# Rows spread by DMA instead of PE, skip term and step size folded into the scores

## Time and profile before

| what | value |
|---|---|
| median of 3 runs | 1815.66 us (1814.56 to 1815.7) |
| profiled execution | 1815.06 us, span 1813.0 us, mean granted PE clock 0.984 |
| PE busy | 1716.9 us, 95% |
| DVE busy | 1071.7 us, 59% |
| POOL busy | 638.6 us, 35% |
| ACT busy | 521.5 us, 29% |
| DMA | 16.90 MB, mean 9 GB/s |

### The profile page before, as it was taken

One profiled execution on the slowest core, in us unless ns is written; L12 is line 12 of the kernel. 1 busy time (PEld: TensorE's weight loads), 2 busy tenths in 40 slices (PEclk: granted clock), 3 DMA queues, 4 the chain that ended last, 5 costly groups with the idle time before them and its releaser, 6 DMA issues.

```text
span 1813.0 us, 27884 instructions
## 1 busy us (share of the span) xinstructions
PE 1716.9 (95%) x9266; PEld 1364.8 (75%) x9266; DVE 1071.7 (59%) x3116; ACT 521.5 (29%) x906; POOL 638.6 (35%) x724
## 2 busy tenths in 40 slices
PE   5589999999999999999999999999999999999997
PEld 3468778787787878778787777878778787777875
DVE  5555656656565665656656565665656656565635
ACT  3342322324132242323324222242323324232120
POOL 4534251423425144251423415143251523425130
PEclk9779999999999999999999999999999999999999
DMA  2300000000000000000000000000000000000000
GB/s 72 103 6 1 7 7 7 7 6 1 6 6 6 6 7 0 7 6 6 7 6 1 6 7 6 6 7 6 1 6 6 7 6 1 6 7 7 1 6 6
DMA packets 22310, 16.90 MB, mean 9 GB/s; under 512 B 1661, under 2 KB 18761, under 8 KB 22217
## 3 DMA queue, kind: packets, MB, share of 16 engines
q1 hardware_dynamic: 22216, 15.99, 2.9%
HBM read 11.80 MB, written 4.19 MB: 9 GB/s over the span
## 4 chain that ended last, share of the span: by engine, by line
PE 65%; issue 19%; POOL 6%; DVE 6%; ACT 2%; DMA 0%; POOLq 0%; DVEq 0%; ACTq 0%; SPq 0%
PE exp_bank L218 14%; PE exp_bank L220 14%; PE exp_bank L219 14%; PE mix_bank L709 3%; PE mix_bank L218 3%; POOL Wt L682 3%; PE mix_bank L219 3%; PE mix_bank L220 3%; PE mix_bank L717 3%; PE mix_bank L733 2%; PE row_bank L894 2%; POOL sp_lo L915 1%; POOL Wt L629 1%; DVE Xd L536 1%; PE mix_bank L672 1%
## 5 line engine op out<-in xcount | busy, mean ns | idle before, releaser
L915 POOL TENSOR_TENSOR sp_lo<-fbuf,sp_hi 128x512 fp32r<-128x512 f32 x192 | 247.5, 1293 | 358.1 <-ACT sp_hi L912 357.8
L218 PE MATMUL exp_bank<-sp_hi,w_hi 128*128 128x512 f32 x768 | 307.0, 400 | 8.2 <-DVE acc L1006 8.2
L218 PE MATMUL exp_bank<-w_hi,sp_hi 128*128 128x512 f32 x768 | 305.2, 397 | 2.0 <-POOL sp_lo L956 2.0
L220 PE MATMUL exp_bank<-sp_hi,w_lo 128*128 128x512 f32 x768 | 304.0, 396 | 0.0
L219 PE MATMUL exp_bank<-sp_lo,w_hi 128*128 128x512 f32 x768 | 303.9, 396 | 0.0
L219 PE MATMUL exp_bank<-w_lo,sp_hi 128*128 128x512 f32 x768 | 300.9, 392 | 0.0
L220 PE MATMUL exp_bank<-w_hi,sp_lo 128*128 128x512 f32 x768 | 300.5, 391 | 0.0
L912 ACT CAST sp_hi<-fbuf 128x512 fp32r<-128x512 f32 x192 | 118.8, 619 | 597.1 <-DVE fbuf L900 589.3
L678 DVE TENSOR_TENSOR_SCAN Wt<-mix_bank,ident 128x512 f32<-128x512 f32 x128 | 156.2, 1220 | 131.1 <-PE mix_bank L672 129.4
L682 POOL TENSOR_TENSOR Wt<-Wt,Gm 128x512 f32<-128x512 f32 x128 | 165.6, 1293 | 155.8 <-DVE Wt L678 155.8
L218 PEld LDWEIGHTS exp_bank<-sp_hi,w_hi 128*128 128x128 f32 x768 | 144.6, 188 | 47.5 <-DVE acc L1006 14.8
(11 more groups left out here) (209 smaller groups left out, 2580.5 us busy)
## 6 DMA issues: line engine op xcount, KB each, us to landing
x_in<-in_x SPq DMA_DIRECT2D x16, 256.0 KB, 2.8
result<-acc SPq DMA_DIRECT2D x16, 256.0 KB, 2.3
fbuf<-in_W1T SPq DMA_DIRECT2D x12, 256.0 KB, 3.8
fbuf<-in_W2T SPq DMA_DIRECT2D x12, 256.0 KB, 2.8
Xd<-in_Wzg SPq DMA_DIRECT2D x1, 512.0 KB, 6.0
Xd<-in_Win SPq DMA_DIRECT2D x1, 324.0 KB, 3.9
wout<-in_Wout SPq DMA_DIRECT2D x1, 256.0 KB
Xd<-in_Wz SPq DMA_DIRECT2D x1, 128.0 KB, 4.4
```

The source lines that it names most:

```text
L218: nc.tensor.matmul(ps, s_hi, m_hi, start=start and j == 0, stop=False)
L220: last = nc.tensor.matmul(ps, s_lo, m_hi, start=False, stop=stop and j == n - 1)
L915: sig("xw_lo", PO.tensor_tensor(sp_lo[:, at, :], wide[e % 2], sp_hi[:, at, :].bitcast(F32), ALU.subtract))
```

## The change

- The router weights, the decay rows and their running products are transposed once by PE, written by DMA to small DRAM tensors (`dw_dram`, `dA_dram`, `cum_dram`) and read back by DMA with every partition getting the same row: `expert_weight`, `seg_row`, `start_row`, on SP's queue, into two buffers each. The products at L672, L690 and L894 are gone, and so are the fp32r splits of the rows.
- The DVE instructions that read a spread row from PSUM now read it from SBUF.
- The step size leaves `Xd` and goes into the scores: ACT makes `Gh` = Gm*delta per head, four instructions of 128x128 (`mix_score_step`); POOL scales `ends` by delta.
- The skip term goes into the scores as well: DVE adds D*identity to `Gh` (`mix_score_skip`); the three products with `wxd` are gone.
- `mix_y` of pair q moves behind the first expert of the next pair, the last one behind all experts; the layer norm of the batch before moves from q = 0 to q = 3.
- b2 is laid out for a single product per batch; its rows are loaded by 48 DMAs in the setup, and the ring of expert weights is refilled from `split_expert_weights`.
- SP gets a nop behind each wait.

```diff
-                    wait(DVE, "a_split", b)
-                    sig("Xd", DVE.tensor_tensor(
-                        Xd[:, c, :].rearrange("p (h n) -> p h n", h=H),
-                        bank_of(f"X{c}")[:, :].rearrange("p (h n) -> p h n", h=H),
-                        delta[:, c, :].unsqueeze(2).to_broadcast([P, H, HD]), ALU.mult))
+                    sig("Xd", DVE.tensor_copy(Xd[:, c, :], bank_of(f"X{c}")[:, :]))
...
         def mix_rates(eng, b):
+                sig("ps_dA", PE.transpose(ps[R1, 0:P], a_rows[:, :, :].rearrange("p h c -> p (h c)"), ident[:, :]))
+                sig("dA", AC.activation(dA_t[R1, :], bank_of("dA")[R1, 0:P], ACT.Exp))
+                sig("ecum", DVE.tensor_tensor_scan(cum_t[R1, :], dA_t[R1, :], upper[R1, P - 1:P].to_broadcast([H * NC, P]),
+                                                   1.0, ALU.mult, ALU.mult))
+            if eng is SP:
+                wait(SP, "dA", b)
+                sig("rates_out", SP.dma_start(dA_dram.rearrange("h (c t) -> (h c) t", t=P)[:, 1:P], dA_t[R1, 1:P]))
+                wait(SP, "ecum", b)
+                sig("rates_out", SP.dma_start(cum_dram.rearrange("h (c t) -> (h c) t", t=P), cum_t[R1, :]))
+                wait(SP, "rates_out", b)
+                seg_row(b, 0)
+                seg_row(b, 1)
+                start_row(b, 0)
+                start_row(b, 1)
+
+        def seg_row(b, h):
+            sig(f"seg_in{h % 2}", SP.dma_start(seg_b[h % 2][:, :], dA_dram[h].partition_broadcast(P)))
+
+        def start_row(b, q):
+            wait(SP, "ps_yq", b if q >= 2 else b.prev(), q - 1 if q >= 2 else None)
+            for j in range(2):
+                sig(f"ctd_in{q % 2}", SP.dma_start(ctd[j * NS:(j + 1) * NS, q % 2, :],
+                                                   cum_dram[2 * q + j, P:T].partition_broadcast(NS)))
...
+        def mix_score_step(eng, b, h):
+            G = Gh[h % 2]
+            if eng is AC:
+                wait(AC, "Gm", b)
+                if h >= 2:
+                    wait(AC, "W", b, h - 1)
+                else:
+                    wait(AC, "W", b.prev())
+                for c in range(NC):
+                    last = AC.activation(G[:, c, :], Gm[:, c, :], ACT.Copy, scale=delta[:, c, h:h + 1])
+                sig("G_dt", last)
+
+        def mix_score_skip(eng, b, h):
+            G = Gh[h % 2]
+            if eng is DVE:
+                wait(DVE, "G_dt", b, h + 1)
+                flat = G[:, :, :].rearrange("p c t -> p (c t)")
+                sig("G_skip", DVE.scalar_tensor_tensor(flat, ident4[:, :], d_b[:, h:h + 1], flat, ALU.mult, ALU.add))
...
         def mix_decay(eng, b, h):
-            if eng is PE:
-                sig("ps_seg", PE.matmul(ps[:, :], sel, rows_d[:, :], start=True, stop=True))
-                sig("scan", DVE.tensor_tensor_scan(W, bank_of(f"seg{h}")[:, :], ident4[:, :], 0.0, ALU.mult, ALU.add))
+                wait(DVE, f"seg_in{h % 2}", b, h // 2 + 1)
+                sig("scan", DVE.tensor_tensor_scan(W, seg_b[h % 2][:, :], ident4[:, :], 0.0, ALU.mult, ALU.add))
+            if eng is SP and h + 2 < H:
+                wait(SP, "scan", b, h + 1)
+                seg_row(b, h + 2)
             if eng is PO:
-                sig("W", PO.tensor_tensor(W, W, Gm[:, :, :].rearrange("p c t -> p (c t)"), ALU.mult))
+                wait(PO, "G_skip", b, h + 1)
+                sig("W", PO.tensor_tensor(W, W, Gh[h % 2][:, :, :].rearrange("p c t -> p (c t)"), ALU.mult))
...
         def mix_from_start(eng, b, q):
-                sig("ctd", DVE.tensor_tensor(ctd[:, q % 2, :], bank_of(f"decb{q}")[:, 0:cols], CT[:, P:T], ALU.mult))
+                wait(DVE, f"ctd_in{q % 2}", b, 2 * (q // 2 + 1))
+                sig("ctd", DVE.tensor_tensor(ctd[:, q % 2, :], ctd[:, q % 2, :], CT[:, P:T], ALU.mult))
...
         def mix_y(eng, b, q):
-                mm3(ps[:, :], [(wxd_hi[:, w], wxd_lo[:, w], xT_hi[:, :], xT_lo[:, :])], stop=False)
...
         def route_rows(eng, b):
+                wait(SP, "dwT", b)
+                sig("dw_out", SP.dma_start(dw_dram.rearrange("e (c t) -> (e c) t", t=P), rows[0:E * NC, :]))
+                wait(SP, "dw_out", b)
+                expert_weight(b, 0)
+                expert_weight(b, 1)
...
         def expert_row(eng, b, e):
-                sig("ps_row", PE.matmul(rb[:, :], sel, rows_s[:, :], start=True, stop=True))
-                sig("xw", DVE.tensor_tensor(wide[e % 2], rb[:, :], x1T, ALU.mult))
+                sig("xw", DVE.tensor_tensor(wide[e % 2], row_b[e % 2][:, :], x1T, ALU.mult))
+            if eng is SP and e + 2 < E:
+                wait(SP, "xw", b, e + 1)
+                expert_weight(b, e + 2)
...
         def body(eng, b, front_next, norm_before=True):
             for q in range(NQ):
+                mix_from_start(eng, b, q)
+                experts(eng, p, [e], ahead)
+                mix_score_skip(eng, b, 2 * q + 1)
+                mix_decay(eng, b, 2 * q + 1)
+                if q < NQ - 1:
+                    mix_score_step(eng, b, 2 * q + 2)
+                if q > 0:
+                    mix_y(eng, b, q - 1)
+                experts(eng, p, [e + 1], ahead)
+                if q == NQ - 1 and norm_before:
+                    expert_norm(eng, p.prev())
                 e += 2
                 if q < NQ - 1:
+                    mix_score_skip(eng, b, 2 * q + 2)
                     mix_decay(eng, b, 2 * q + 2)
+                    mix_score_step(eng, b, 2 * q + 3)
-                mix_y(eng, b, q)
             experts(eng, p, range(e, E), ahead)
+            mix_y(eng, b, NQ - 1)
...
         def setup(eng):
+                for e in range(E):
+                    at = B2ROW + e * NC
+                    for c in range(NC):
+                        SP.dma_start(b2_sb[at + c:at + c + 1, c, :], b2[e:e + 1, :]).then_inc(sems["small"], 16)
+                SP.wait_ge(sems["pad"], 6)
+                SP.dma_start(dA_dram.rearrange("h (c t) -> (h c) t", t=P), cum_t[0:H * NC, :]).then_inc(sems["zero"], 16)
...
         def router_product(eng):
+            if eng in (SP, DVE):
+                eng.wait_ge(sems["zero"], 16)
+            if eng is PE:
+                PE.wait_ge(sems["small"], 16 * (5 + E * NC))
```

More of the change, by code:

```diff
@@ L30 @@
 NR = 3
-B2ROW = 32
-DTROW = 64
-LOROW = 32
+WCOLS = 32
+B2ROW = E * NC
 LN_EPS = 1e-5
@@ L115, in layer_program @@
         Gm = sb("Gm", [P, NC, P])
+        Gh = [sb(f"Gh{n}", [P, NC, P]) for n in range(2)]
         Wt = sb("Wt", [P, 2, 2 * T])
@@ L119, in layer_program @@
         ctd = sb("ctd", [P, 2, T - P])
-        rates = ctd[:, :, :].rearrange("p a b -> p (a b)")[:, 0:T]
+        dA_t, cum_t = sb("dA_t", [P, P]), sb("cum_t", [P, P])
+        seg_b = [sb(f"seg_b{n}", [P, T]) for n in range(2)]
         zg = sb("zg", [P, NQ, T])
         dt_s = sb("dt_s", [P, 6, NC * H])
-        delta, a = sb("delta", [P, NC, H]), sb("a", [P, NC, H])
+        delta, a_rows = sb("delta", [P, NC, H]), sb("a_rows", [P, H, NC])
+        a = a_rows[:, :, :].rearrange("p h c -> p c h")
         a_hi, a_lo = sb("a_hi", [P, NC, H], F32R), sb("a_lo", [P, NC, H], F32R)
@@ L178, in layer_program @@
         product("stored", 1, 16)
+        product("dw_out", 1, 16)
+        product("rates_out", 2, 16)
+        for n in range(2):
+            product(f"row_in{n}", E // 2, 16)
+            product(f"seg_in{n}", H // 2, 16)
+            product(f"ctd_in{n}", NQ, 16)
         sems = {n: ctx.enter_context(nc.semaphore("set_" + n)) for n in
                 ("mix_w", "win", "wbdt", "small", "decay_par", "ring0", "ring1", "ring2", "ring3",
-                 "w_hi", "w_lo0", "w_lo1", "masks", "cast", "chain", "chain_d", "alog", "ps_r", "router", "pad")}
+                 "w_hi", "w_lo0", "w_lo1", "masks", "cast", "chain", "alog", "ps_r", "router", "pad", "zero")}
         waited = {}
@@ L566, in mix_rates @@
                 ps = mix_bank(b, "dA")
-                for c in range(NC):
-                    last = PE.matmul(ps[RATES, tok(c)], a[:, c, :], ident[:, :], start=True, stop=True)
-                sig("ps_dA", last)
+                sig("ps_dA", PE.transpose(ps[R1, 0:P], a_rows[:, :, :].rearrange("p h c -> p (h c)"), ident[:, :]))
             if eng is AC:
                 wait(AC, "ps_dA", b)
-                wait(AC, "cum_lo", b.prev())
-                wait(AC, "ps_yq", b.prev())
-                sig("dA", AC.activation(rates[RATES, :], bank_of("dA")[RATES, :], ACT.Exp))
@@ L960, in expert_b2 @@
             if eng is PE:
-                wait(PE, "xw", b)
-                for c in range(NC):
-                    last = PE.matmul(rb[:, tok(c)], rows[:, tok(c)], b2_sb[:, :], start=True, stop=True)
-                sig("ps_b2", last)
+                wait(PE, "dwT", b)
+                sig("ps_b2", PE.matmul(rb[:, :], rows[:, :], b2_sb[:, :, :].rearrange("p c d -> p (c d)"), start=True, stop=True))
             if eng is DVE:
```

216 lines of the change are left out of this document (75 added, 141 removed).

## The result

| | before | after |
|---|---|---|
| median, us | 1815.68 (1814.56 to 1816.82, 4 runs) | 1832.86 (1830.59 to 1834.58, 4 runs) |
| ratio, 95% interval | | 1.0094 [1.0076, 1.0111] |
| span of the profiled execution, us | 1813.0 | 1831.4 |

Slower, inside the range; the forecast moved the time by 8 us, the chip by 17. Most of what was forecast of the head pairs came true. The slowdown itself came from a place where I had written "as late as now", and not from the terms that made the forecast slower.

What follows compares the result with a forecast made beforehand. PE bounds the kernel before; after the change the SBUF port shared by DVE and POOL takes PE's saving back. 1813.0 + 15 x 0.0 + 12 - 2.6 = 1822.4 us span, median 1824, range 1680 to 1860.

Steps and rivals of the forecast that it cites:

- The port: Head pairs: DVE instructions with two SBUF inputs and POOL's exclude each other, so a pair needs 9.2 us; chance 0.57.
- The skip addition's holding of 0.54: Head pairs: each skip addition on DVE keeps POOL off for 0.54 us, taken from the nearest row; 1.07 at the scan's rate.
- PE's saving: Per body: removed row and skip products and shorter ones save PE 9.0 us; a pair would need 7.5 us of PE.
- the rival that PE stays the bound: Head pairs: scans and skips don't hold the port, -7.5 to -10 us per body, 1690 us; chance 0.17.
- DVE restarts as late as now: Start of a pass: DVE was assumed to begin as late as in the kernel before, no change.
- The sum of the body: One pass: -0.8 us, against eight handovers at 0.1 us of semaphore each, gives 0.0; bounds -10 and +4.
- Expert 2 at 664.0, 2.0 us earlier: First stretch of a body: the rates' transposition, 3 row products and the earlier row bring expert 2 about 2.0 us forward.
- Batch 0, +12: Batch 0: b2's loads delay the router's product by 5 to 12 us, four pairs add 4; bounds +3 to +22.
- The last mixture, -2.6: End of the kernel: the last mixture loses 11 row products, -2.6 us.
- The late row: Router row by DMA arrives late, `xw` 0 holds up PE's first expert: +1.5 us a pass, 1847 us; chance 0.17.
- The clock: Head pairs: PE less busy, its granted clock falls to 0.77, +60 us, 1885 us; chance 0.09.
- The signs: Right: slower scans, `xw`, POOL products, PE busy about 85%, period 107; wrong: period below 102, router's product before 33 us.

Runs made afterwards that it cites:

- e6: The changed kernel, with ACT copying the identity once a pass into the router's PSUM bank, where scans and skip additions read it; 1732.55 us, ratio 0.9548.
- e5: The changed kernel with one more small DVE copy in the setup and nothing else; 1815.11 us, ratio 1.0008.
- e2: The changed kernel with two rotating PSUM banks instead of three, the third holding the identity for scans and skip additions; 1813.93 us, ratio 0.9998.
- e3: The changed kernel with two rotating PSUM banks instead of three and the identity still in SBUF; 1903.01 us, ratio 1.0483.
- e4: The kernel before with step size and skip term folded into the scores and outputs one expert later, rows still with PE and PSUM; 1785.81 us, ratio 0.9842.
- e7: The kernel before with one more small DVE copy in the setup; 1813.9 us, ratio 1.0003.
- e1: The changed kernel with expert 2's row sent after the loop's restart instead of just before it; 1830.06 us, ratio 1.0087.
- e9: The changed kernel with four small DVE copies added in the setup; 1816.84 us, ratio 1.0004.

## Why the prediction was right in its course and short in size

- *The port, right.* A pair was priced at 9.2 us and, with handovers, a pass at no change; measured are 9.48 a pair and 47.49 us from expert 2 to the last output, where the hand schedule had 711.3 - 664.0 = 47.3. e6 against e5, and e2 against e3, show the mechanism by taking it away. The skip addition's holding of 0.54, the nearest row's, was good enough: 0.74 us alone.
- *PE's saving, right.* e4 returns the skip products at 0.23 each; e6, freed of the port, has passes of 102.7 us, 5.6 below before, where the rival that PE stays the bound had 7.5 to 10 less. The difference lies in the waits that e6 still has: without PE's waits a pass takes 97.2 us there and 105.7 in before, 8.5 less, where 9.0 were forecast.
- *The step that failed: "DVE restarts as late as now".* In its place the restart took 4.25 us instead of 3.20. It cost 1.0 us in E to T of each of the 12 passes behind a jump back, 4.5 us for the clock in three of them, and 2.1 more at the entry to the loop. e5 prices it: 1832.86 - 1815.11 = 18 us. With it undone, 13 passes last 1.3 us less than before, 0.1 a pass, against the 0.0 of the forecast.
- *The sum of the body, right by luck.* By its own terms it was -0.9 (711.3 against 712.2) - 0.3 + 0.8 for handovers = -0.4 a body, or -6 us in all; I had added -0.9 and -0.3 up to -0.8. Expert 2 then came 0.7 later and B to E 0.4 longer than forecast, which made up for it. (In the last line, too, 1824.5 and 0.6 make 1825 and not 1824.)
- *Expert 2 at 664.0, 2.0 us earlier: too much.* Counted from the transposition it came 1.3 earlier (10.22 us against 11.51), as T to S shows too (-1.25). What kept the other 0.7 I did not isolate.
- *Batch 0, +12: too much; measured +5.5.* Two errors of opposite sign. The loads of b2 were priced by the rows of other loads, at 0.43 to 0.60; they took 0.30, and the router's product came 3.7 us earlier instead of 5 to 12 later. The four pairs cost more: from the router's product to the first E 92.8 us instead of 83.6, +9.2 for the +4 forecast. And the port, which the +4 was for, is the smaller part of it. From the first to the fourth outputs it is 23.8 us in before, 30.1 in after and still 28.1 in e6, where skips and scans read PSUM: 2.0 of 6.3. The rest is in e4 too, whose first E comes 9.7 later than before.
- *The last mixture, -2.6:* from the fifteenth pass's E to the end it was -5.5 in after and -3.9 in e5; of the last mixture by itself -5.0, or -1.8 from e7 to e5, which is too uneven to say more than the sign. Smaller terms: B to E grew by 0.07 us and was to shrink by 0.3; expert 4's row came 13 us later than I had put it, and little hung on it (at most about 1 us a pass).
- *The rivals.* PE as the bound fell by the rows above. The late row fell: B to E is 46.71 against 46.64, and `xw` 0 waits for nothing in any pass of the loop. The clock did fall, but almost without a price. In after it went to the level 1.2 GHz for a few us, in the 3.2 us wait of the pairs or up to 1.5 us behind it, in 5 of the 13 loop passes (in e5 in 11), and S to B took the same 44.5 to 44.6 us with and without, as the port set the pace:

```profile
1008.66:1053.22 44.56, 37.24 (x233) 27.33 (x232) 41.27 (x44) 18.50 (x46) 29.44 (x18) 0.96 0.31 85
1119.46:1164.04 44.58, 35.76 (x234) 26.28 (x233) 41.27 (x44) 18.50 (x46) 29.45 (x18) 1.00 0.27 85
```

- *The signs.* Of the signs of being right nearly all came: scans up to 2.3 us, `xw` at 1.21 on average, POOL's products at 1.56 and 1.68, PE busy 87%; only the waits before the outputs did not, PE waits before the experts alone. Two of the signs of being wrong came as well, a DMA as the releaser of `xw` (expert 4) and the router's product before 33 us; they belong to the two terms above, not to the port.

In sum: batch 0 gave 6.5 us less than forecast, the end 2.9 less, the first and the 13 loop passes 18.4 more; 18.4 - 6.5 - 2.9 = 9.0, the distance of 1831.4 from 1822.4. The size was off by a term that I had set to zero without a bound. The direction was luck: the forecast was slower because of batch 0 and the end, +12 - 2.6, and these two together came to 0.0 (+5.5 - 5.5); with the restart as late as now, as in e5, the change makes no difference.

## What to carry to other kernels

Before an operand is moved from PSUM to SBUF to relieve one engine, count for each DVE instruction whether it would then read two SBUF inputs while POOL works: here the same scan lasts 1.20 or 1.61 us on average by the place of an identity matrix, and with the skip addition's that is 82 us of the kernel. Where the change cuts PE's work but another resource takes it back, a constant in an idle PSUM bank may be all that is wanted. And after any edit of a looped kernel, compare the gap at the loop's restart engine by engine before the edit itself is judged: a shift of one instruction was worth 1%.

## What the runs showed that I had not expected

- DVE's jump back took 3.12 to 3.28 us (median of a kernel) in nine kernels and 4.21 to 4.25 in three (after, e1, e3), with no semaphore shown that it waits for. One 6-column copy ahead of the loop changes the level, and the long restarts all have a second packet of the instruction queue in the gap. That the place of the instructions is behind it fits e5, e7 and e9; what in the place decides is open.
- The length of a wait does not tell whether PE's granted clock falls behind it. At the transposition it fell behind 2.06 us and stayed up behind 1.83 in after, but fell behind 1.82 and stayed up behind 2.04 in e1; around the 3.2 us wait in the pairs it fell in 5 of 13 passes of after and in 11 of e5. What it costs depends on who sets the pace: nothing in these pairs, 0.6 us a time in e6, 1.3 to 1.8 from T to S.
- A DMA of one short row of b2 takes SP 0.30 us to issue, where others in the setup took 0.42 to 0.72. The size is not what decides: the 256 KB row of an expert, sent alone, took 0.32. What does is open.
